# Four graph layers on one core: TensorE's signals moved to drains, and a new order in the second attention

## The chip, the core and the metric

The kernel runs on one core of one Trainium2 chip. A core has TensorE (matmuls, results in PSUM), VectorE, ScalarE and GpSimd for arithmetic, SyncE for issuing transfers, and 16 DMA engines. The engines run their own instruction streams and meet through semaphores: an instruction may wait until a semaphore has reached a number, and may raise one when it is done. The metric is the device time of one execution in microseconds.

## The reference: what is computed

A graph of 6250 nodes with 128 features and 106250 edges (sorted by target) goes through four layers, each followed by a residual and a layer norm:

```python
edge_index = jnp.stack([src, dst])
deg = jnp.maximum(segment_sum(ones(dst.shape), dst), 1.0)
x = _layernorm(x + _L0_gnn_ref(x, ..., deg ** -0.5, src, dst, edge_type_40))  # 40 relations, weights 128x128 each
x = _layernorm(x + _L1_gnn_ref(x, edge_index, W, att_src, att_dst, ...))       # attention, 4 heads of 64
x = _layernorm(x + _L2_gnn_ref(x, edge_index, W_proj, score_src, ...))         # attention, 4 heads of 32
x = _layernorm(x + _L3_gnn_ref(x, edge_index))                                 # 6 rounds of capsule routing
```

The second attention, which the change rearranges, is this:

```python
scores = leaky_relu(s_src[src] + s_tgt[tgt], 0.2)
exp_scores = exp(scores - max(scores))
denom = segment_sum(exp_scores, tgt)
att = exp_scores / (denom[tgt] + 1e-16)
out = segment_sum(proj[src] * att[:, :, None], tgt)
```

## The kernel before

Edges are laid out in 880 chunks of 128 slots, each chunk with targets of one tile of 128 nodes. Work goes by groups of CQ = 4 chunks, so there are NQ = 220 groups, and most buffers are rings of RING = 4 groups. `sweep(eng, stages, ...)` writes one engine's program: for each iteration q it runs the listed steps in their order, a step `(off, fn)` on group q + off. Each engine has its own sweep, and they meet through semaphores alone. A step's waits stand at its head.

Five stages issue indirect transfers from GpSimd, one for each chunk:

- *Relation products* (line 490 on): GpSimd scatters 831 columns of edge records into `rec_tab` (L472). Beside it, TensorE makes y = x W_r for all nodes and 40 relations: for each of 50 tiles a transpose (L491), which ScalarE reads into `xt` (L484), and ten matmuls of 512 columns (L497), each of which VectorE adds into `y_out` (L509) and SyncE stores to `y_tab`. TensorE may be four products ahead of VectorE (`s_yc`).
- *First gather* (`total`, L827): rows of `y_tab` are gathered (L562 `ring<-y_tab`), summed by one-hot matmuls, four a group, and added by VectorE to `acc` (L813). SyncE stores one-hots for later stages.
- *Source maxima* of the first attention: GpSimd gathers (L1035 `ring_m`), ScalarE packs score parts (L1088), TensorE's `turn` transposes them (L1108), ScalarE copies the lines (L1096), TensorE's `spread` makes for each chunk four narrow matmuls (L1118) and a wide one (L1121), and VectorE takes the maximum (L1067). The gathered rows are stored to `k_tab`. GpSimd may reuse a buffer when ScalarE has packed it and the store has landed.
- *Second attention* (`attend_once`): GpSimd gathers (L562 `ring_e<-t_tab`); it may reuse a buffer when VectorE's `message` has read it. `expand` (L1532) and `turn` (L1542) are matmuls on loaded one-hots `ohts`; VectorE's `sent` (L1440) sums the expansion, `score` (L1449, L1451, L1454) ends in `lane_top`; TensorE's `lanes` (L1548) transposes that, VectorE's `top` (L1458, L1461) takes the running maximum, TensorE's `spread_top` (L1552) spreads it, ScalarE's `shift` (L1504, L1507, L1511) negates it and takes the exponentials, VectorE's `message` (L1468) multiplies, TensorE's `total` (L1561) sums the messages by target, and VectorE's four `add` steps (L1484, L1487, L1490) put the sums into `acc`.
- *First routing round*: GpSimd gathers (L1827), SyncE stores the rows, TensorE does `total` (L1963), `turn` (L1953) and `expand` (L1942), VectorE product, sums, shares, messages (L1845 to L1881), ScalarE exponentials and copies (L1904 to L1922).

Between them lie the first attention proper (`attend`) and, at the end, five later rounds (L2060 to L2239), whose transfers are all SyncE's.

On the kernel before, every signal of TensorE is raised by the last matmul of a step, as in

```python
for c in range(CQ):
    last = nc.tensor.matmul(sums(s, c), hots[:, s, c, :], msg[:, s, c, :],
                            start=True, stop=True)
last.then_inc(s_sum, 1)
```

## Time and profile before

| what | value |
|---|---|
| median of 3 runs (lowest to highest) | 11336.08 us (11329.6 to 11339.88) |
| the profiled execution | 11339.56 us |
| its span, first to last instruction | 11337.8 us |
| mean granted clock of TensorE | 0.703 |
| busy: TensorE, VectorE, ScalarE, GpSimd | 60%, 57%, 22%, 57% |

No engine is busy two thirds of the time, so the page's shares alone say little: they are averages over stages with different limits. The profile calls TensorE's matmuls PE, its weight loads PEld, VectorE DVE, ScalarE ACT, GpSimd POOL and the issuing of a queue POOLq or SPq. An idle time is put down to a releaser: an engine and line, a DMA, "issue" (nothing that the profile shows) or "remote" (a signal that it can't match to an instruction's end). Names in rows drop buffer and stage numbers: `ring_e` is that of the second attention in rows of L562.

### The profile page before, as it was taken

The numbers are of one execution on the slowest core, as the hardware profiler recorded it, in microseconds if no ns is written. First come the engines' busy times: TensorE is split into PE (matmuls) and PEld (weight loads), VectorE is DVE, ScalarE is ACT, GpSimd is POOL, SyncE is SP. The second block draws the span as 40 slices with busy tenths as digits, with TensorE's granted clock in tenths as the row PEclk, the third lists the DMA queues.
The fourth block names the chain that finished last, engine by engine and source line by source line (L and its number), as shares of the span: only waits on it lengthen the run. The fifth ranks groups of instructions, "written<-read, shape, count | busy, mean of one in ns | idle before, by whom it ended". The sixth has DMA issues, their size and how long they took to land. (4 is left out here: it accounts for less than half of the span.)

```text
span 11337.8 us, 161595 instructions
## 1 busy us (share of the span) xinstructions
PE 6767.9 (60%) x41381; PEld 5071.3 (45%) x41382; DVE 6482.6 (57%) x18631; ACT 2515.4 (22%) x6766; POOL 6430.9 (57%) x5741
## 2 busy tenths in 40 slices
PE   4422256333337777688745555345444698898986
PEld 3200022333323333344434444244444698898986
DVE  7411135555555555677754444534444688888888
ACT  0000000000010000022211111133333455555554
POOL 0477732777726666444235555255555587787876
PEclk9755577555565555599865555577776899999998
DMA  0111135555546666655322222233333566666664
GB/s 22 58 47 46 46 145 184 117 115 117 113 80 172 176 175 176 167 181 182 115 53 62 61 61 62 40 97 97 95 97 96 145 210 186 186 210 187 209 186 149
DMA packets 1109223, 1395.56 MB, mean 123 GB/s; under 512 B 277691, under 2 KB 974351, under 8 KB 1108111
## 3 DMA queue, kind: packets, MB, share of 16 engines
q1 hardware_dynamic: 955182, 1090.46, 31.1%
q0 software_dynamic: 153312, 296.65, 12.9%
q8 instruction: 304, 4.98, 0.2%
q14 instruction: 425, 3.47, 0.1%
HBM read 1002.58 MB, written 383.96 MB: 122 GB/s over the span
## 5 line engine op out<-in xcount | busy, mean ns | idle before, releaser
L562 POOL DMA_INDIRECT ring_e<-t_tab,src_row x880 | 832.4, 946 | 825.6 <-DVE msg_e L1468 424.1
L1827 POOL DMA_INDIRECT z_r<-x_tab,src_row x880 | 839.4, 954 | 805.6 <-DVE msg_r L1865 405.1
L562 POOL DMA_INDIRECT ring<-y_tab,y_row x880 | 881.7, 1002 | 726.4 <-DVE ring L783 356.5
L472 POOL DMA_INDIRECT rec_tab<-pay,row_i x831 | 842.3, 1014 | 694.5 <-POOLq L202 402.1
L2227 PE MATMUL ps<-u,wide_r 128*128 x9280 | 1141.4, 277 | 126.2 <-issue 88.7
L2239 PE MATMUL ps<-msg_r,hots_r 128*128 128x128 f32 x9280 | 1150.8, 277 | 105.4 <-POOL msg_r L2060 104.7
L2060 POOL TENSOR_TENSOR msg_r<-zo_r,share_r 128x1024 f32<-128x1024 f32 x580 | 1122.8, 1936 | 87.5 <-DVE share_r L2119 13.7
L2227 PEld LDWEIGHTS ps<-u,wide_r 128*128 128x128 f32 x9280 | 1093.0, 194 | 128.2 <-issue 128.2
L2239 PEld LDWEIGHTS ps<-msg_r,hots_r 128*128 128x128 f32 x9280 | 1083.2, 192 | 138.4 <-POOL msg_r L2060 137.7
L1035 POOL DMA_INDIRECT ring_m<-t_tab,src_row x880 | 850.5, 966 | 516.7 <-ACT slot_parts_m L1088 262.9
L497 PE MATMUL ps<-w,xt 128*128 128x512 f32 x1000 | 607.2, 747 | 821.8 <-issue 503.7
L2068 POOL TENSOR_TENSOR prod_r<-prod_r 128x512 f32<-128x512 f32 x580 | 735.1, 1267 | 437.4 <-DVE prod_r L2091 425.1
L509 DVE TENSOR_TENSOR y_out<-ps,rf_b 128x512 f32<-128x512 f32 x500 | 330.9, 689 | 1124.8 <-remote 794.4
L827 PE MATMUL ps<-ring,hots 128*128 128x129 f32 x1760 | 458.6, 442 | 835.4 <-issue 561.1
L1067 DVE TENSOR_REDUCE high_m<-ps 128x4 f32<-128x512 f32 x880 | 588.9, 685 | 623.4 <-PE ps L1121 348.3
L827 PEld LDWEIGHTS ps<-ring,hots 128*128 128x128 f32 x1760 | 394.1, 329 | 900.1 <-issue 679.0
L497 PEld LDWEIGHTS ps<-w,xt 128*128 128x128 f32 x1000 | 207.4, 228 | 1202.8 <-issue 672.4
L1118 PE MATMUL ps<-lines_m,pick_m 48*128 48x128 bf16 x3520 | 530.5, 304 | 350.2 <-DVE high_m L1067 273.5
L2091 DVE TENSOR_TENSOR prod_r<-ps,zo_r 128x1024 f32<-128x1024 f32 x580 | 707.9, 1221 | 33.3 <-PE ps L2227 30.8
L2130 DVE TENSOR_TENSOR u_sum<-ps,u_sum 128x128 f32 x2320 | 667.4, 288 | 89.5 <-PE ps L2239 40.2
L1561 PE MATMUL ps<-msg_e,hots_e 128*128 128x132 f32 x1760 | 468.2, 447 | 333.9 <-DVE msg_e L1468 333.9
L1963 PE MATMUL ps<-msg_r,hots_r 128*128 128x128 f32 x1760 | 341.4, 355 | 509.9 <-DVE msg_r L1865 395.2
(320 smaller groups left out, 13430.4 us busy)
## 6 DMA issues: line engine op xcount, KB each, us to landing
zo_r<-zo_tab SPq DMA_DIRECT2D x2320, 192.0 KB
y_tab<-y_out SPq DMA_DIRECT2D x250, 512.0 KB
k_tab<-ring_m SPq DMA_DIRECT2D x220, 520.0 KB
ring_e<-k_tab SPq DMA_DIRECT2D x220, 520.0 KB
ohts_e<-oht_tab SPq DMA_DIRECT2D x440, 128.0 KB
zo_tab<-z_r SPq DMA_DIRECT2D x220, 256.0 KB
dl_b<-dl_tab SPq DMA_DIRECT2D x220, 128.0 KB
oht_tab<-ohts SPq DMA_DIRECT2D x220, 128.0 KB
```

The source lines that it names most:

```text
L472: nc.gpsimd.indirect_dma_start(out=rec_tab, out_offset=bass.IndirectOffsetOnAxis(ap=row_i[:, j:j + 1], axis=0), in_=pay[:, j, :], in_offse ...
L497: nc.tensor.matmul(ps[:, n % 4, :], xt[:], w0[:, 4 * g:4 * g + 4, :], start=True, stop=True).then_inc(s_y, 1)
L562: nc.gpsimd.indirect_dma_start(out=ring[:, s, c, 0:width], out_offset=None, in_=table, in_offset=bass.IndirectOffsetOnAxis(ap=rows[:, q * ...
L827: last = nc.tensor.matmul(ps[:, (s % 2) * CQ + c, 0:W], hots[:, s, c, :], ring[:, s, c, :], start=True, stop=True)
L1035: nc.gpsimd.indirect_dma_start(out=ring[:, s, c, :], out_offset=None, in_=t_tab, in_offset=bass.IndirectOffsetOnAxis(ap=src_row[:, q * CQ ...
L1827: nc.gpsimd.indirect_dma_start(out=z[:, s, c * D:(c + 1) * D], out_offset=None, in_=x3_tab, in_offset=bass.IndirectOffsetOnAxis(ap=src_row ...
L2060: nc.gpsimd.tensor_tensor(msg[:, g % WR].rearrange("p c (k d) -> p c k d", d=CD), z_of(g).rearrange("p c (k d) -> p c k d", d=CD), share[: ...
L2068: nc.gpsimd.tensor_tensor(prod[:, :, 0:CD // 2], prod[:, :, 0:CD // 2], prod[:, :, CD // 2:CD], ALU.add).then_inc(s_half, 1)
L2091: v.tensor_tensor(prod[:].rearrange("p (c k) d -> p c (k d)", k=CAPS), up, z_of(g), ALU.mult).then_inc(s_prod, 1)
L2130: v.tensor_tensor(t, ps[:, 4 + g % 2, a * D:(a + 1) * D], t, ALU.add)\
L2227: last = nc.tensor.matmul(ps[:, 2 * (g % 2) + c // 4, c % 4 * D:(c % 4 + 1) * D], wide[:, g % WR, c, :], u[:, bass.ds(tiles[g % NO % 4 * O ...
L2239: last = nc.tensor.matmul(ps[:, 4 + g % 2, c // 2 * D:(c // 2 + 1) * D], hots[:, g % WR, c, :], msg[:, g % WR, c, :], start=c % 2 == 0, st ...
```

## The change

It does two things.

First, in the five stages with indirect transfers TensorE's matmuls and transposes raise no semaphore any more. Behind them stands a drain, an instruction of TensorE that raises it: 550 in the relation products (one for each of 50 transposes and 500 products), 220 in the first gather, 5 a group in the source maxima and in the second attention, 3 a group in the first round. The stages without indirect transfers keep their signals.

Second, the second attention is put in another order. TensorE's total runs one group late and stands between this group's `lanes` and `spread_top`; `expand` and `turn` work two groups ahead, not one, and stand last. VectorE's adds are two groups late, not one, and `sent` stands just ahead of `message`. ScalarE does `shift` ahead of `hot`, the latter one group ahead. SyncE loads the one-hots two groups ahead. `spread` is put into another bank of PSUM.

```diff
@@ relation products
-                        nc.tensor.transpose(ps[:, 7, 0:P], xs[:], ident[:]).then_inc(s_xtp, 1)
+                        nc.tensor.transpose(ps[:, 7, 0:P], xs[:], ident[:])
+                        nc.tensor.drain().then_inc(s_xtp, 1)
...
                             nc.tensor.matmul(ps[:, n % 4, :], xt[:], w0[:, 4 * g:4 * g + 4, :],
-                                             start=True, stop=True).then_inc(s_y, 1)
+                                             start=True, stop=True)
+                            nc.tensor.drain().then_inc(s_y, 1)
@@ first gather
-                        last.then_inc(s_sum, 1)
+                        nc.tensor.drain().then_inc(s_sum, 1)
@@ source maxima: turn, spread
-                            nc.tensor.transpose(turned(s), parts[:, s, :], ident_b[:])\
-                              .then_inc(s_turn, 1)
+                            nc.tensor.transpose(turned(s), parts[:, s, :], ident_b[:])
+                            nc.tensor.drain().then_inc(s_turn, 1)
...
-                                                 far[:].rearrange("p h e -> p (h e)"), start=False, stop=True)\
-                                  .then_inc(s_spread, 1)
+                                                 far[:].rearrange("p h e -> p (h e)"), start=False, stop=True)
+                                nc.tensor.drain().then_inc(s_spread, 1)
@@ second attention (attend_once)
                 def spread(s):
-                    return ps[:, 6 + s % 2, 3 * P:3 * P + 1]
+                    return ps[:, (s % 2) * CQ // PER, 3 * P:3 * P + 1]
...
-                        sweep(sp, [(1, hots_in)], straight=True)
+                        sweep(sp, [(2, hots_in)], straight=True)
...
-                        tiles = Tiles(DVE_ENGINE, -1)
+                        tiles = Tiles(DVE_ENGINE, -2)
...
-                        sweep(dve, [(1, sent), (-1, add(0)), (0, score), (-1, add(1)), (-1, add(2)),
-                                    (0, top), (-1, add(3)), (0, message)], tiles, straight=True)
+                        sweep(dve, [(0, score), (-2, add(0)), (-2, add(1)), (0, top), (-2, add(2)),
+                                    (-2, add(3)), (1, sent), (0, message)], tiles, straight=True)
...
-                        sweep(act, [(0, hot), (0, shift)], straight=True)
+                        sweep(act, [(0, shift), (1, hot)], straight=True)
...
-                        tiles = Tiles(PE_ENGINE, 1)
+                        tiles = Tiles(PE_ENGINE, 2)
...
-                            last.then_inc(s_sum, 1)
-                        sweep(pe, [(1, expand), (1, turn), (0, lanes), (0, spread_top), (0, total)], tiles, straight=True)
+                            nc.tensor.drain().then_inc(s_sum, 1)
+                        sweep(pe, [(0, lanes), (-1, total), (0, spread_top), (2, expand), (2, turn)], tiles, straight=True)
```

The other signals of the second attention (`s_exp`, `s_turn`, `s_row`, `s_bc`) and the three of the first round (`s_exp`, `s_turn`, `s_sum`) are moved to a drain in the same way. Line numbers of the changed kernel are one to three higher.

On TensorE, one group in the middle of the second attention stood like this before (`exp_n` with `ohts` is the expansion, which comes four times, `ident_b` the transposes, then lanes, spread and total; drains are no rows here):

```order
L1532 ISA
L1532 MATMUL ps<-exp_n_e2,ohts_e2 128x12
...
L1542 MATMUL ps<-ident_b,ohts_e2 128x128 x4
L1548 MATMUL ps<-ident,lane_top_e2 1x128
L1552 MATMUL ps<-run_top_e2,one_row_e2 128x1
L1561 MATMUL ps<-msg_e2,hots_e2 128x132 x4
```

and stands like this now:

```order
L1550 MATMUL ps<-ident,lane_top_e2 1x128
L1564 MATMUL ps<-msg_e2,hots_e2 128x132 x4
L1555 MATMUL ps<-run_top_e2,one_row_e2 128x1
L1534 ISA
L1534 MATMUL ps<-exp_n_e2,ohts_e2 128x12
...
L1544 MATMUL ps<-ident_b,ohts_e2 128x128 x4
```

The four sums (`msg_e2`, now of the group before) moved from behind the spread to ahead of it, and the expansion from the head to the end.

On VectorE, the same group before (`sent`, an add and its copy, the three of score, further adds, the two of top, the message; repeated adds are left out):

```order
L1440 TENSOR_REDUCE sent_e2<-ps 128x16
...
L1484 SCALAR_TENSOR_TENSOR acc<-acc,fade_e2,ps 128x132
...
L1449 TENSOR_TENSOR sc_e2<-ring_e2,sent_e2 128x16
L1451 SCALAR_TENSOR_TENSOR sc_e2<-sc_e2 128x16
L1454 TENSOR_REDUCE lane_top_e2<-sc_e2 128x1
...
L1487 TENSOR_TENSOR acc<-ps,acc 128x132
...
L1458 TENSOR_REDUCE quad_top_e2<-ps 1x1
L1461 TENSOR_TENSOR run_top_e2<-quad_top_e2,run_top_e2 1x1
...
L1468 TENSOR_TENSOR msg_e2<-ring_e2,msg_e2 128x4x128
```

and now:

```order
L1451 TENSOR_TENSOR sc_e2<-ring_e2,sent_e2 128x16
L1453 SCALAR_TENSOR_TENSOR sc_e2<-sc_e2 128x16
L1456 TENSOR_REDUCE lane_top_e2<-sc_e2 128x1
...
L1486 SCALAR_TENSOR_TENSOR acc<-acc,fade_e2,ps 128x132
...
L1460 TENSOR_REDUCE quad_top_e2<-ps 1x1
L1463 TENSOR_TENSOR run_top_e2<-quad_top_e2,run_top_e2 1x1
...
L1442 TENSOR_REDUCE sent_e2<-ps 128x16
L1470 TENSOR_TENSOR msg_e2<-ring_e2,msg_e2 128x4x128
```

`sent` moved from the head of the group to just ahead of the message, and score is now the first thing behind the message of the group before.

## Rows read from the trace of the kernel before

**Rows 1.** The page's strip of 40 equal slices: TensorE's granted clock, in tenths.

```profile
PEclk9755577555565555599865555577776899999998
```

**Rows 2.** Busy time by stage: PE, PEld, DVE, ACT, POOL, PEclk, DMA share, GB/s.

```profile
405.00:1545.00 1140.00, 339.47 (x442) 106.90 (x442) 143.16 (x208) 11.51 (x44) 842.25 (x831) 0.56 0.16 54
1545.00:1862.00 317.00, 275.54 (x608) 109.24 (x608) 187.74 (x292) 13.59 (x57) 0.00 (x0) 0.97 0.59 242
1896.00:3168.00 1272.00, 458.33 (x1760) 394.08 (x1760) 670.68 (x1754) 0.00 (x0) 881.69 (x880) 0.50 0.53 113
3347.00:4734.00 1387.00, 1015.11 (x4620) 418.14 (x4620) 762.00 (x1993) 90.39 (x441) 850.51 (x880) 0.50 0.65 172
5770.00:7260.00 1490.00, 796.38 (x4180) 638.76 (x4180) 685.28 (x3311) 253.58 (x882) 832.38 (x880) 0.50 0.28 60
7374.00:8894.00 1520.00, 734.84 (x4400) 663.70 (x4400) 630.30 (x1756) 543.33 (x2863) 839.43 (x880) 0.70 0.37 96
```

**Rows 3.** Who GpSimd waited for: us in total, times, longest.

```profile
POOL ring_e L562 <- DVE msg_e L1468: 424.1, 216, 7.1
POOL z_r L1827 <- DVE msg_r L1865: 405.1, 88, 6.8
...
POOL ring_m L1035 <- ACT slot_parts_m L1088: 262.9, 100, 16.3
POOL z_r L1827 <- issue: 257.3, 791, 5.3
...
POOL ring_m L1035 <- issue: 253.7, 780, 3.9
POOL ring_e L562 <- issue: 204.0, 663, 0.5
...
POOL ring L562 <- remote: 109.3, 38, 3.6
```

**Rows 4.** Timeline in the relation products: start, us, instruction, idle before it.

```profile
907.66 0.28 ACT L484 ACTIVATE xt<-ps 128x128 f32<-128x128 f32 x1 [58.33 <-remote]
...
923.07 0.69 DVE L509 TENSOR_TENSOR y_out<-ps,rf_b 128x512 f32<-128x512 f32 x1 [4.91 <-remote]
...
923.81 2.08 PE L497 MATMUL ps<-w,xt 128*128 128x512 f32 x2 [4.18 <-DVE y_out L509]
```

**Rows 5.** Timeline in the first routing round: TensorE's weight loads.

```profile
8029.41 0.19 PEld L1942 LDWEIGHTS ps<-unit,wide_r 128*128 128x128 f32 x1 [1.23 <-issue]
...
8030.82 0.19 PEld L1942 LDWEIGHTS ps<-unit,wide_r 128*128 128x128 f32 x1 [1.23 <-issue]
```

**Rows 6.** Timeline of one group in the second attention.

```profile
6404.70 0.17 DVE L1449 TENSOR_TENSOR sc_e<-ring_e,sent_e 128x16 f32<-128x16 f32 x1
...
6405.34 0.08 PEld L1548 LDWEIGHTS ps<-ident,lane_top_e 128*1 128x1 f32 x1 [1.01 <-DVE lane_top_e L1454]
...
6406.45 0.50 PEld L1552 LDWEIGHTS ps<-run_top_e,one_row_e 1*128 1x128 f32 x2 [1.04 <-DVE run_top_e L1461]
...
6407.07 0.17 ACT L1504 ACTIVATE neg_e<-ps 128x1 f32<-128x1 f32 x1 [5.44 <-issue]
...
6407.80 0.69 DVE L1468 TENSOR_TENSOR msg_e<-ring_e,msg_e 128x512 f32<-128x512 f32 x1 [1.07 <-ACT msg_e L1511]
...
6408.55 2.12 PE L1561 MATMUL ps<-msg_e,hots_e 128*128 128x132 f32 x8 [1.51 <-DVE msg_e L1468]
...
6410.25 0.42 PEld L1532 LDWEIGHTS ps<-exp_n_e,ohts_e 128*128 128x128 bf16 x4
...
6411.32 0.16 DVE L1449 TENSOR_TENSOR sc_e<-ring_e,sent_e 128x16 f32<-128x16 f32 x1
```

**Rows 7.** Timeline in the source maxima: TensorE's narrow and wide matmuls.

```profile
3902.20 0.34 PEld L1118 LDWEIGHTS ps<-lines_m,pick_m 48*128 48x128 bf16 x4 [0.44 <-issue]
...
3902.74 0.61 PE L1121 MATMUL ps<-far_m,others_m 128*128 128x512 bf16 x1
...
3903.28 0.34 PEld L1118 LDWEIGHTS ps<-lines_m,pick_m 48*128 48x128 bf16 x4 [0.44 <-DVE high_m L1067]
```

More of the change, by code:

```diff
@@ L1535, in expand @@
                                     start=True, stop=True)
-                            last.then_inc(s_exp, 1)
+                            nc.tensor.drain().then_inc(s_exp, 1)
                         def turn(q, s):
@@ L1543, in turn @@
                                                            ohts[:, s, c * P:(c + 1) * P], ident_b[:])
-                            last.then_inc(s_turn, 1)
+                            nc.tensor.drain().then_inc(s_turn, 1)
                         def lanes(q, s):
                             pe.wait_ge(s_lt, q + 1)
-                            nc.tensor.transpose(lane_row(s), lane_top[:, s, :], ident[:]).then_inc(s_row, 1)
+                            nc.tensor.transpose(lane_row(s), lane_top[:, s, :], ident[:])
+                            nc.tensor.drain().then_inc(s_row, 1)
                         def spread_top(q, s):
                             pe.wait_ge(s_rt, q + 1)
-                            nc.tensor.matmul(spread(s), one_row[:], run_top[0:1, s:s + 1], start=True, stop=True)\
-                              .then_inc(s_bc, 1)
+                            nc.tensor.matmul(spread(s), one_row[:], run_top[0:1, s:s + 1], start=True, stop=True)
+                            nc.tensor.drain().then_inc(s_bc, 1)
                         def total(q, s):
@@ L1945, in expand @@
                                             start=True, stop=True)
-                                    last.then_inc(s_exp, 1)
+                                    nc.tensor.drain().then_inc(s_exp, 1)
                                 def turn(q, s):
@@ L1954, in turn @@
                                                                    ohts[:, s, c * P:(c + 1) * P], ident_b[:])
-                                    last.then_inc(s_turn, 1)
+                                    nc.tensor.drain().then_inc(s_turn, 1)
                                 def total(q, s):
@@ L1964, in total @@
                                                                 msg[:, s, c * D:(c + 1) * D], start=True, stop=True)
-                                    last.then_inc(s_sum, 1)
+                                    nc.tensor.drain().then_inc(s_sum, 1)
                                 sweep(pe, [(-1, total), (1, turn), (2, expand)], tiles, straight=True)
```

## The prediction

> **What bounds the kernel now.** I first read the page's strip of 40 slices, then cut the span into stages, then asked each stage which engine's waits add up to its length. Five stages issue indirect transfers from GpSimd, and the granted clock of TensorE is low just there [rows 1]. They take 1140 + 317 us (relation products, with the scatter of the records and after it), 1272 (first gather), 1387 (source maxima), 1490 (second attention) and 1520 us (first routing round) [rows 2]: 7126 of 11337.8 us. In each, GpSimd does the same thing: 880 gathers, or 831 scatters, of 0.95 to 1.01 us busy each (the busy sums in [rows 2] over their counts), about 0.3 us of issue between them, and waits for others [rows 3]. Busy time, issue and waits make 850.5 + 253.7 + 262.9 = 1367 us in the source maxima, 832.4 + 204.0 + 424.1 = 1460 in the second attention and 839.4 + 257.3 + 405.1 = 1502 in the first round. A wait that vanished would leave the usual 0.3 us, so 100, 216 and 88 waits leave 233, 359 and 379 us to win, and the first gather's 38 of 109.3 us leave 98. The floor is then 1134, 1101 and 1123 us, for 220 groups of four transfers each 5.0 to 5.2 us. That floor is the first thing to keep in mind.
>
> The second is what holds it up. In the relation products VectorE adds 29 tiles of ten in the 317 us behind the scatter and only 21 in the 1140 us beside it (608 and 442 TensorE records, 21 to a tile) [rows 2]. At 923 us it has waited 4.91 us for a product and works 0.69 on it, 5.6 us for each; TensorE starts another product at 923.81, 0.05 us after that add ended, so VectorE's signals are prompt and TensorE is ready ahead; ScalarE sat 58.33 us before it could read one transpose at 907.66 [rows 4]. So the signals of matmuls arrive late, in a queue. In the first round TensorE's own loads step slowly: 8029.41 to 8030.82 is 1.41 us for a load and a matmul, 0.7 us for each [rows 5]; 5.6 us is eight such steps. The second attention has no such delay: there ScalarE starts at 6407.07, 0.62 us after the load of the tiny matmul it reads, in every group alike, and the 6.62 us of a group (6404.70 to 6411.32) is a plain chain [rows 6].
>
> **Drains.** 50 + 500 signals in the relation products, 220 in the first gather, 1100 in the source maxima, 1100 in the second attention and 660 in the first round move from the matmul to a drain behind it: 3630 drains. No row shows one. What they can take away are the late signals; what they cost is overlap, since the next weights may load only when the array is empty. 
> - *Relation products.* When signals are prompt a tile takes about 11 us: 29 in 317 us [rows 2]. Fifty are 550 us, half of the 1140 us that GpSimd scatters in. The stage then ends with the scatter and the 317 us behind it go. Bounds: 0 (delay stays) to 365 (842.3 us busy and 0.3 us between 831 scatters are 1092 us, 48 less than the 1140). I take 317.
> - *First gather.* One signal a group; VectorE's 670.68 us and TensorE's 458.33 are 3.0 and 2.1 us a group and fit under 5.2 [rows 2]. Bounds 0 to 98, taken 98.
> - *Source maxima.* Four spreads a group, each four narrow matmuls and a wide one, 1.08 us apart; from the first load to the wide one's end is 3902.20 to 3903.35, 1.15 us [rows 7]. With a drain the next load starts behind that end; I add 0.1 us for the drain, estimated from the 0.05 us in which a signalled engine starts, twice. TensorE is busy 1015 us or 4.6 a group [rows 2], so the transpose takes some 0.3 beside four times 1.08. Four times 1.25 and 0.4 make 5.4 us: TensorE, at its lower level here (granted 0.50, 1.2 GHz), becomes the limit over GpSimd's 5.15. 220 x 5.4 = 1188 against 1367: 175 taken, bounds 0 (6.2 us a group, drains of 0.3 us) and 233.
> - *First round.* 379 us of waiting. TensorE is busy 734.84 us in 220 groups, 3.3 us each, at a mean grant of 0.70; all at the low level (0.50) that would be 4.7, with three drains 5.0 [rows 2]. GpSimd's 5.1 stays the limit, near a tie: 355 taken, bounds 0 and 379.
>
> Here a rule speaks against the change. In the second attention a total's next load starts 1.70 us after the total's first load (6408.55 to 6410.25) though the matmuls end at 2.12 [rows 6]: 0.4 us of overlap that a drain takes. The Trainium skill, page "TensorE: Matmul & The Clock Gate", section "Single matmul latency", gives about 183 ns at the low clock for what a matmul hides when others follow; by it 3630 drains would take 660 us of TensorE time, by the row's 0.4 us 1450. Neither is added, because except in the source maxima it lies under GpSimd.
>
> **The second attention's new order.** Before, on one chain: score, lanes' transpose, top, spread, ScalarE's three, message, sums (2.12 us), expansion, `sent`, score. After, the sums of q-1 run on TensorE behind the lanes of q, the expansion is a group ahead. The loop, by [rows 6]: score to the transpose's load 0.64 (6404.70 to 6405.34); transpose 0.37; drain 0.1; sums 2.12; drain 0.1; spread to ScalarE 0.62 (6406.45 to 6407.07) and 0.03; ScalarE to message 0.73; message to the next score 0.61 (0.69 less the overlap of neighbours). That is 5.3 us. `quad_top`, `run_top` and the adds lie beside the 2.12 of the sums (VectorE is busy 3.1 us a group in all [rows 2]); the next group's transposes and expansions follow the spread and lie beside ScalarE and the message. 220 x 5.3 = 1166 us against 220 x 6.62 = 1456: 290 taken. Bounds: 359 (GpSimd's floor) and 200 (drains at 0.25 us each: 5.7 us a group). The gather transfers wait for the message of three groups ago and will be asked for at once; the loads of `ohts` come one group earlier with four buffers, 128 KB each, at a DMA share of 0.28.
>
> **Sum.** 317 + 98 + 175 + 355 + 290 = 1235 us. The profiled execution took 11339.56 us around a span of 11337.8, and the median is 11336.08, 0.03% lower. 11339.6 - 1235 = 10105, so 10100 us.
>
> **The rivals.**
> - *All prompt, as above* (0.60): 9900 to 10400.
> - *Cured in part* (0.20): delays stay where TensorE does most per signal and stores are heavy. For it: in the relation products each matmul advances by 0.7 us steps, which a drain need not change. Relation products and first round unchanged give 10100 + 317 + 355 = 10770; the source maxima alone, 10275. Range 10400 to 10900.
> - *Drains don't touch the delay, only the new order counts* (0.10): 11340 - 290 = 11050, 10900 to 11310. For it: in [rows 5] the loads themselves, which raise nothing, are late, so completion as such may be slow, with or without a signal.
> - *Slower* (0.07): the drain waits for the same slow completion, and now everything behind it on TensorE stands still. The Trainium skill, page "PSUM — Partial Sum Buffer", section "Engine vs sequencer instructions", says that drain waits for the engine to go fully idle. One delay of 0.7 us per drain serial in source maxima and first round, where groups have 5 and 3: 220 x (5 + 3) x 0.7 = 1230 us on top of 5.4 and 5.1 us, thus 8.9 and 7.2 us a group against 6.2 and 6.8 now; +590 and +90, less 290: 11730. It decides where 290 us are lost against now: 0.33 us for each of the 880 spreads, over the 0.16 that brings a group of the maxima from 5.4 back to 6.2.
> - *Nothing measurable* (0.03): order's gain and drains' loss cancel.
>
> **How the numbers follow.** The likeliest is 10100. Its case and the partial cure hold 8 in 10, so the range is 9900 to 10900. The low end is all five floors: 11340 - 365 - 98 - 233 - 359 - 379 = 9906. 0.2% is 23 us, about what a measurement tells from no change. Faster 0.90, same 0.03, slower 0.07.
>
> **What would show it.** Relation products ending within some 20 us of the last scatter; VectorE's 4.9 us waits gone; ScalarE's 58 us waits gone. GpSimd at 5.0 to 5.3 us a group in all but the source maxima, and there TensorE's loads following each wide matmul by 0.1 us, a group in 5.4. In the second attention a group in 5.3 us with the sums between the lanes' transpose and the spread. From 8925 us on (the later rounds) nothing changes its length. Wrong: loads on TensorE that still step by 0.7 or 1.4 us beside indirect transfers; a drain that delays the next load by more than 0.3 us; or transfers that take longer once they are asked for sooner (the source maxima already have a DMA share of 0.65).

## The result and the profile after

The changed kernel takes **11408.82 us** (median of 5 runs, 11395.09 to 11430.54), the kernel before 11339.88 us beside it (5 runs, 11329.6 to 11344.11). The ratio is 1.0063, with a 95% interval of 1.0049 to 1.0077: 0.6% slower, where 10100 us had been forecast.

One thing has to be known for the numbers below. The experiments ran on several chips, and the kernel before took 11342 to 11347 us on some of them (11340 beside the change), but 10247 to 10253 us on others. One chip of each kind was used two times, some 40 minutes apart, and was of the same kind both times. So every experiment is read against the kernel before on its own chip, and I call the two kinds **late chips** and **prompt chips**, for what their traces turned out to show.

First the stages of the profile after, in the columns of [rows 2]. Its span is 11428.4 us; the profiled execution was the slowest of the five, 22 us over their median, so the stages add up to somewhat more than the medians differ by:

```profile
405.00:1542.00 1137.00, 412.76 (x419) 101.64 (x420) 137.49 (x199) 11.10 (x42) 829.28 (x831) 0.51 0.15 52
1542.00:1949.00 407.00, 353.37 (x632) 94.70 (x631) 208.07 (x302) 14.07 (x59) 0.04 (x1) 0.96 0.47 194
1983.00:3250.00 1267.00, 456.13 (x1760) 394.25 (x1760) 668.69 (x1754) 0.00 (x0) 882.95 (x880) 0.50 0.52 114
3426.00:4856.00 1430.00, 1053.85 (x4590) 415.61 (x4590) 799.77 (x1973) 89.31 (x440) 837.27 (x881) 0.50 0.61 167
5904.00:7390.00 1486.00, 931.04 (x4180) 694.64 (x4180) 686.15 (x3309) 253.87 (x881) 832.37 (x880) 0.50 0.26 60
7508.00:8981.00 1473.00, 948.47 (x4388) 788.77 (x4389) 636.97 (x1752) 542.90 (x2862) 836.07 (x880) 0.57 0.38 99
```

Against [rows 2], the work behind the scatter grew from 317 to 407 us, and the first gather (1267) and the second attention (1486) stayed where they were. The windows have margins of some us, so the stages' costs are better taken from the starts of GpSimd's first transfers in them, of before in the first line view and of after in the second (count, minimum, median and maximum in ns, first and last start):

```profile
L562 POOL DMA_INDIRECT ring<-y_tab,y_row x880: 942/947/1362, 1896.9 to 3147.5; - x176
L1035 POOL DMA_INDIRECT ring_m<-t_tab,src_row x880: 943/949/3143, 3347.3 to 4712.9; - x176
L562 POOL DMA_INDIRECT ring_e<-t_tab,src_row x880: 942/947/1004, 5770.4 to 7229.9; - x176
L1827 POOL DMA_INDIRECT z_r<-x_tab,src_row x880: 942/947/1467, 7374.0 to 8874.9; - x176
```

```profile
L564 POOL DMA_INDIRECT ring<-y_tab,y_row x880: 942/947/1382, 1983.6 to 3233.9; - x176
L1037 POOL DMA_INDIRECT ring_m<-t_tab,src_row x880: 943/949/3147, 3426.6 to 4824.9; - x176
L564 POOL DMA_INDIRECT ring_e<-t_tab,src_row x880: 942/947/997, 5904.5 to 7365.5; - x176
L1830 POOL DMA_INDIRECT z_r<-x_tab,src_row x880: 942/947/1449, 7507.9 to 8962.5; - x176
```

The lag of after behind before is 86.7, 79.3, 134.1 and 133.9 us at these four starts and 90.6 at the end of the span. So the relation products cost 87 us, the first gather gives 7, the source maxima (with what follows up to the second attention) cost 55, the second attention gives nothing and the first round 43. Of the five terms of the sum, 317, 98, 175, 355 and 290, none arrived.

The reason is in the waits of the profile after (us in total, times, longest), where PEq is TensorE's sequencer and PEq L500, L1111, L1125 and L1556 are the new drains:

```profile
DVE y_out L511 <- PEq L500: 1121.9, 465, 20.0
ACT lines_m L1098 <- PEq L1111: 1075.2, 174, 21.9
...
ACT neg_e L1506 <- PEq L1556: 801.6, 126, 7.3
...
DVE high_m L1069 <- PEq L1125: 533.1, 667, 13.8
...
POOL ring_e L564 <- DVE msg_e L1470: 351.0, 109, 8.3
...
POOL z_r L1830 <- DVE msg_r L1868: 326.8, 136, 8.0
```

VectorE still waits for the products, only that the wait now ends with the drain. The drains themselves stand in the views of their lines, with minimum, median and maximum in ns:

```profile
L500 PEldq DRAIN  x500: 942/1100/6198, 422.3 to 1945.8; - x167
```

```profile
L1566 PEldq DRAIN  x220: 1925/2102/5147, 5933.5 to 7386.2; - x110
```

A drain behind a product lasts 1.10 us where all is well and up to 6.2 where it isn't; one behind the sums of the second attention, which are 2.10 us of matmuls, up to 5.1. A drain waits for the late completion like everyone else. (A matmul's end is modelled in the profile, so no row tells whether the array works slowly or finishes in time and reports late. "Late completion" stands for both.)

The second attention shows when that happens. Before, nothing was late there. The timeline after, of two groups (start, us, instruction, idle before it):

```profile
6502.99 0.95 POOL L564 DMA_INDIRECT ring_e<-t_tab,src_row  x1 [3.71 <-DVE msg_e L1470]
...
6503.87 2.10 PE L1564 MATMUL ps<-msg_e,hots_e 128*128 128x132 f32 x8 [0.23 <-DVE acc L1486]
...
6506.05 0.50 PEld L1555 LDWEIGHTS ps<-run_top_e,one_row_e 1*128 1x128 f32 x2 [0.38 <-issue]
...
6506.74 0.95 POOL L564 DMA_INDIRECT ring_e<-t_tab,src_row  x1 [0.31 <-issue]
...
6508.38 0.95 POOL L564 DMA_INDIRECT ring_e<-t_tab,src_row  x1 [0.69 <-issue]
...
6510.12 2.10 PE L1564 MATMUL ps<-msg_e,hots_e 128*128 128x132 f32 x8 [0.23 <-DVE acc L1489]
...
6512.13 0.96 POOL L564 DMA_INDIRECT ring_e<-t_tab,src_row  x1 [0.31 <-issue]
...
6513.73 0.49 PEld L1555 LDWEIGHTS ps<-run_top_e,one_row_e 1*128 1x128 f32 x2 [1.82 <-issue]
...
6516.13 0.94 POOL L564 DMA_INDIRECT ring_e<-t_tab,src_row  x1 [3.04 <-DVE msg_e L1470]
```

In the first group GpSimd has just paused 3.71 us; the sums end at 6505.97 and TensorE goes on at 6506.05. The loop is then the one that was forecast: 5.4 us from message to message. In the second, GpSimd's four transfers follow the last four after only 0.69 us; the sums end at 6512.22, but the next load starts at 6513.73, 0.6 us after GpSimd's last transfer of that run ended (6513.09), and the group takes 7.7 us. Then GpSimd has to wait for messages (3.04 us), and the next group is prompt again. Through most of the stage groups of 5.4 us alternate with late ones of 7.7 to 8.4, and their mean is the old 6.6 us.

Counted over all 220 drains of L1566: where at most four transfers had begun in the 8 us before the drain did (104 drains), the mean is 2.1 us; with five (58 drains) it is 4.1 and with six (58) 3.3. In the first gather the same count gives 2.07 us for the 66 drains with at most four, and 5.1, 5.9 and 9.1 us for the 154 with five, six and seven. It is no rule for the whole kernel: of the drains behind products (L500), the eight with three or four such transfers took 3.8 to 5.5 us, so what went before counts too (experiment 9 comes back to it).

**Theory A**, from this: on such a chip TensorE's completions come late, drain or not, while GpSimd issues indirect transfers one behind the other, and short pauses in them keep it from happening. Where TensorE is late, GpSimd soon has to wait, and that is its pause: the stages settle at the length at which GpSimd pauses enough, whatever is won in their chains. **Theory B**, the rival: the drains themselves bring the lateness into the second attention.

### The profile page after: what moved, and what is told of

The parts are those of the page before. It is cut to its first block and busy times, and to the rows that moved or that the text cites. A ratio compares the mean times of both kernels' runs of the same rounds, so it can differ in the third digit from the quotient of the medians.

```text
span 11428.4 us, 165225 instructions
## 1 busy us (share of the span) xinstructions
PE 7313.4 (64%) x41381; PEld 5234.5 (46%) x41382; DVE 6549.6 (57%) x18631; ACT 2518.2 (22%) x6766; POOL 6402.9 (56%) x5741
## 5 line engine op out<-in xcount | busy, mean ns | idle before, releaser
L2242 PE MATMUL ps<-msg_r,hots_r 128*128 128x128 f32 x9280 | 1152.3, 277 | 104.9 <-POOL msg_r L2063 104.3
L498 PE MATMUL ps<-w,xt 128*128 128x512 f32 x1000 | 746.9, 837 | 689.8 <-issue 655.0
L1204 POOL TENSOR_TENSOR msg_e<-ring_e,msg_e 128x768 f32<-128x768 f32 x220 | 324.1, 1473 | 558.0 <-ACT msg_e L1310 558.0
L2182 ACT ACTIVATE wide_r<-zo_r 128x1024 f32<-128x1024 uint8 x580 | 605.5, 1044 | 86.1 <-PE ps L2230 60.2
```

Source lines behind the costliest of these rows:

```text
L498: nc.tensor.matmul(ps[:, n % 4, :], xt[:], w0[:, 4 * g:4 * g + 4, :], start=True, stop=True)
L2242: last = nc.tensor.matmul(ps[:, 4 + g % 2, c // 2 * D:(c // 2 + 1) * D], hots[:, g % WR, c, :], msg[:, g % WR, c, :], start=c % 2 == 0, st ...
```

## The experiments

**1. The order alone.** No drain anywhere; the edit on the kernel before is the order's part of the change:

```diff
-  sweep(pe, [(1, expand), (1, turn), (0, lanes), (0, spread_top), (0, total)], ...)
+  sweep(pe, [(0, lanes), (-1, total), (0, spread_top), (2, expand), (2, turn)], ...)
```

> The kernel before with the second attention's new order and no drain. Theory A (GpSimd's indirect transfers, once they follow each other without a pause of some 1.7 us, make TensorE's completions late, with a drain or without): the faster order lets GpSimd close its pauses, completions become late in about every second group, and the stage keeps 1440 to 1480 us; the total is within 40 us of before. Theory B (the drains make the delay in the second attention): groups of 5.3 us, the stage 1170 to 1200 us, the total about 11050.

This met a prompt chip: 9913.43 us against 10253.16 (ratio 0.9675, 0.9659 to 0.9691). There the second attention takes what GpSimd needs and no more:

```profile
405.00:1476.00 1071.00, 472.92 (x1050) 185.75 (x1050) 322.49 (x500) 24.84 (x101) 795.84 (x831) 0.74 0.34 129
1512.00:2663.00 1151.00, 447.71 (x1740) 389.69 (x1741) 665.89 (x1739) 0.00 (x0) 880.62 (x880) 0.50 0.56 124
2855.00:3991.00 1136.00, 954.04 (x4471) 412.53 (x4558) 783.28 (x1962) 88.18 (x435) 852.31 (x880) 0.50 0.77 208
5048.00:6169.00 1121.00, 729.09 (x4132) 616.09 (x4132) 682.33 (x3254) 250.06 (x870) 848.93 (x880) 0.50 0.34 79
6306.00:7446.00 1140.00, 705.87 (x4372) 650.55 (x4372) 624.50 (x1731) 538.10 (x2835) 860.48 (x880) 0.79 0.49 127
```

All 50 tiles of products are done beside the scatter (x1050), and each gather stage runs at GpSimd's floor of 5.1 to 5.2 us a group. These are the floors of the forecast, without a single drain. On its own this run can't part A from B: on a prompt chip nothing is late. The granted clock is 0.50 (the 1.2 GHz level) in three of the five rows here too, so the low clock is not what makes completions late.

**2. The drains alone**, in the old order (prompt chip).

```diff
-  sweep(pe, [(0, lanes), (-1, total), (0, spread_top), (2, expand), (2, turn)], ...)
+  sweep(pe, [(1, expand), (1, turn), (0, lanes), (0, spread_top), (0, total)], ...)
```

> The kernel after with the second attention's old order; all 3630 drains stay. Theory A: relation products, source maxima and first round as in the kernel after (88 and 54 us longer, 46 us shorter than before); the second attention keeps GpSimd's pause of about 1.9 us in each group, so no completion is late there, and its chain grows by five drains of about 0.05 us: 6.62 to 6.9 us a group, 1460 to 1515 us. Total 11400 to 11490. Theory B: the second attention shows late completions here too, over 7 us a group.

10608.03 us against 10253.16 (1.0352, 1.0335 to 1.0370): no lateness (every drain of L1566 lasts 2.13 us), but drains are dear in themselves. The source maxima take 1206 us, 5.5 a group, and the second attention 1704, which is 7.7 a group in place of 6.6. I had expected 0.05 us a drain. A group now takes 7.5 us, and every fourth 8.6. TensorE in one of the plain groups:

```profile
6011.72 1.82 PEld L1564 LDWEIGHTS ps<-msg_e,hots_e 128*128 128x128 f32 x8 [1.62 <-DVE msg_e L1470]
...
6014.17 0.48 PEld L1534 LDWEIGHTS ps<-exp_n_e,ohts_e 128*128 128x128 bf16 x4 [0.63 <-issue]
```

From the sums' first load to the expansion's it is 2.45 us, where it was 1.70 [rows 6]. The sequencer sets registers for each of the expansion's four matmuls; before, it did so from 0.13 us after the sums' start on (6408.68), beside them, and now it does so when the drain of 2.13 us has ended, and the four matmuls take 0.56 us in place of 0.30. Every fourth group has one instruction of the sequencer more there:

```profile
L591 PEldq TENSOR_LOAD <-chunk_tile x1: 1109/1109/1109, 6005.3 to 6005.3; - x1
```

In that group the sums start at 6003.10; the sequencer waits in the drain, loads the next tile numbers into its registers at 6005.3 for 1.11 us, and the expansion starts at 6006.72, 3.62 us after the sums. The old order without drains has this load too, in one group of four, and takes the same 1.92 us from the sums' first matmul to the expansion's with the load and without: there it is hidden behind the sums. So of the 1.1 to 1.2 us that a group grows by, some 0.9 come with the drains in every group, and 0.3 are the load of 1.11 us in one of four.

**3. Two probes with drains**: half the gathers of the second attention are left out from the fifth group on, and the scatters wait behind the products.

```diff
-  for c in range(CQ):                              # gathers, second attention
+  for c in range(2 if q >= RING else CQ):
...
   def _(pool):                                     # relation products
+      pool.wait_ge(s_y, NTP * GRP)
```

> The kernel after with two probes. In the second attention GpSimd issues only two of a group's four gathers from the fifth group on (half of the gathered rows are left out, so the sums are of stale rows); in the relation products GpSimd's scatters wait until all products are made. Theory A: with two gathers a group GpSimd pauses 2.8 us in every group, so no completion is late and the new order shows its own loop of 5.3 to 5.4 us, the stage 1170 to 1200 us; the products take 11 us a tile from the first to the last, 550 us for 50, and behind them the scatters take 831 x 1.265 = 1050 us. Theory B (drains as such): every second group of the second attention still takes 7.7 us, and products with a drain stay at 58 us a tile part of the time.

Prompt chip again, 10767.5 us (one run). The new order's own loop with drains is 1235 / 220 = 5.6 us: 5.4 in three groups and 6.2 to 6.4 in every fourth, the one with the load of tile numbers. Products with drains take 654 us in all, 12.8 a tile, over the 11 that I had expected.

**4. Pauses in the scatter alone.**

```diff
   for j in range(EJ):
+      if j % 4 == 0 and 0 < j // 4 * 7 <= NTP * GRP:
+          pool.wait_ge(s_yc, j // 4 * 7)
```

> The kernel before with one edit in the relation products: after every fourth scatter GpSimd waits until seven more products are added, as long as there are products. Theory A: four scatters are 5.1 us and seven products 7 to 8 us, so GpSimd pauses 2 to 3 us in every such stretch, no completion is late, 50 tiles take 500 to 550 us with about 285 scatters beside them, and the 546 left take 690 us: the stage is 1200 to 1240 us in place of 1455, total 11080 to 11130. If it is the mere presence of indirect transfers or of the stores beside them that makes completions late, products stay slow, GpSimd waits for them, and the stage is over 2000 us.

On the prompt chip this only costs: 10424.02 against 10253.16 (1.0172, 1.0155 to 1.0189), the stage 1244 us. The trace also shows the old order of the second attention on a prompt chip: 6.6 us a group, as on the late chip of [rows 6]. So nothing was late there in the old order on either kind.

**5. The kernel after again**, unchanged (late chip).

> The kernel after, unchanged, beside the kernel before. The kernel before took 10253 us in the experiments so far, against 11340 beside the first run of the kernel after, and no completion was late in them. Theory C: late completions belong to the machine the kernels run on, not to the kernel. If before takes about 10250 here, after shows no late completion, the source maxima take 1205 us (70 longer than without drains), the second attention 1230 us, and the total is 10080 to 10120, 1.5% under before. If before takes about 11340, after is 11400 again, with the stages of its first profile. Rival: late completions come with the kernel after's drains as such; then after is above 11300 even where before takes 10250.

11429.09 against 11341.89 (1.0081, 1.0064 to 1.0098), with GpSimd's stages starting within 9 us of where they did in the first profile. So the result on record is that of a late chip. The kernel after was never run on a prompt one; from stages that were, counted from stage start to stage start, it would be 9913 less 10 (first gather), plus 77 (source maxima) and 11 (first round) as between experiments 1 and 2, plus 116 (second attention, between 1 and 3): about 10107 against 10250. That is a sum over three traces, not a run.

**6. Order and pauses, without drains** (the same late chip).

> Two edits on the kernel before: the second attention's new order without drains, and in the relation products GpSimd waits for seven more added products after each four scatters. Theory C with no late completions (before at about 10250): the order gives 335 us, the pauses cost 170 as in the run of the pauses alone, total 10085. With late completions (before at about 11340) and theory A: the pauses keep the products at 11 us a tile and the stage at 1240 us in place of 1455, the second attention closes GpSimd's pauses and stays at 1440 to 1480 us, total 11100 to 11150. If late completions need no dense transfers, the relation products stay slow and the total is over 11500.

11083.0 against 11341.89 (0.9772, 0.9756 to 0.9789). Its two stages:

```profile
405.00:1645.00 1240.00, 471.86 (x1050) 184.81 (x1050) 322.04 (x500) 24.90 (x101) 798.34 (x831) 0.71 0.30 112
5551.00:6980.00 1429.00, 730.57 (x4137) 617.30 (x4138) 676.58 (x3260) 250.41 (x870) 832.27 (x880) 0.50 0.27 63
```

With GpSimd made to pause, all 50 tiles are made beside the scatter, as on a prompt chip: 1240 us in place of 1457. And the order without a single drain still takes 1429 us where the prompt chip takes 1121: groups of 4.7 and 5.4 us alternate with late ones of 6.9 to 8.4. Theory B falls: lateness comes into the second attention with the faster order, not with the drains. Of the 290 us forecast for the order, 61 arrive without drains (1490 to 1429), and the drains take them away again (1486 in the profile after).

**7. The probes of 3 without drains** (the same late chip).

> No drains, the second attention's new order with two of four gathers a group left out from the fifth group on (its sums are of stale rows), and the scatters behind the relation products. The same two probes with drains gave 1234 us (5.6 us a group) in the second attention and 11 to 13 us a tile of products. If the drains on the chain hold the new order's loop, it is faster without them: 4.7 to 5.0 us a group, 1030 to 1100 us. With late completions about (before at about 11340) and theory A, both probes are prompt all the same, since GpSimd pauses; if completions are late here too, the pauses don't cure.

Both were prompt. The rows (all products in 532 us with no transfer about; two gathers a group, 1080 us or 4.9 a group):

```profile
405.00:937.00 532.00, 473.09 (x1050) 188.04 (x1050) 319.65 (x498) 24.96 (x101) 0.00 (x0) 0.97 0.62 254
5915.00:6995.00 1080.00, 728.93 (x4131) 615.91 (x4131) 672.61 (x3250) 249.96 (x870) 423.84 (x448) 0.50 0.22 56
```

The same loop without drains is 0.7 us a group shorter than in experiment 3.

**8. Shorter pauses, and drains in the first round** (late chip): the kernel of 6 with six products in place of seven, and the drains of L1949, L1958 and L1968.

> The kernel before with three edits: the second attention's new order without drains, drains in the first routing round alone, and in the relation products GpSimd waits for six more added products after each four scatters (a period of 6.2 to 6.6 us, a pause of 1.2 to 1.5). On a machine with late completions (before at about 11340), by theory A: if a pause of 1.2 to 1.5 us is still enough, the relation products take 1190 to 1210 us (1240 with seven), and the total is 11000 to 11040 with the first round's 46 us; if it is too short, the products are late in part and the stage is 1250 to 1450. On one without (before at about 10250): order -335, pauses +120, drains +10, total 10050.

10967.95 against 11347.04 (0.9666, 0.9653 to 0.9679). The relation products' stage is 1184 us, so shorter pauses, most of them of 0.7 to 2 us, are enough; the first round takes 1453 us in place of the 1520 of [rows 2] without drains. The whole is 32 us under the range that I had expected.

**9. Doses of pauses** (the same late chip as 8). Before scatter j GpSimd waits for the count of added products in a table:

```diff
+  for n, a in [(4, 7), (4, 6), (4, 5), (8, 12), (8, 10), (16, 21)]:
+      for k in range(1, 78 // a + 1):
+          waits[j0 + k * n] = a0 + k * a
+      j0, a0 = j0 + 78 // a * n, a0 + 78 // a * a
...
+      if j in waits:
+          pool.wait_ge(s_yc, waits[j])
```

> How long a pause, after how many transfers. No drains. In the relation products GpSimd's scatters wait in six stretches of 75 to 78 products each: four scatters to seven products, four to six, four to five, eight to twelve, eight to ten, sixteen to twenty-one (prompt products take 1.0 us each, a scatter 1.27, so the pauses are about 2.2, 1.2, 0.4, 2.2, 0.3 and 1.1 us). In the second attention (new order) GpSimd waits before every second group alone and then issues eight gathers in a row. Theory A with late completions about (before at 11340): the stretches with the pauses of 2.2 us are prompt (7.2 us and 12.5 us a period), those with 0.3 to 0.4 us fall to 5.6 us a product; the pause of 1.2 us lies near the edge, prompt if over half of 1.7. In the second attention the pause is per eight gathers: if the run of eight stays prompt, a group takes 5.8 us or less (1280 us), else 6.5 as before (1430). If late completions depend on the share of time and not on the pause, four to seven and eight to twelve differ from four to six alone by their share (5.1 of 7.2, 10.1 of 12.5, 5.1 of 6.2).

VectorE's busy time and count of adds in the six stretches and in the one without waits behind them:

```profile
424.00:506.00 82.00, 48.81 (x77) 0.99 0.61 241
506.00:587.00 81.00, 50.49 (x79) 0.98 0.65 252
587.00:675.00 88.00, 49.07 (x76) 0.96 0.59 228
675.00:756.00 81.00, 46.43 (x72) 0.98 0.61 241
756.00:840.00 84.00, 44.94 (x70) 0.90 0.55 214
840.00:917.00 77.00, 40.94 (x64) 0.93 0.55 214
917.00:1166.00 249.00, 44.00 (x65) 0.62 0.20 71
```

Per product that is 1.06, 1.03, 1.16, 1.13, 1.20, 1.20 and, without waits, 3.8 us. I had expected four to five and eight to ten to be late all through; they lose a tenth or two. The doses that GpSimd took are not those of the table, though. Where the products ran ahead of the count it didn't wait at all: the trace has runs of 20 transfers in the stretch of four to five and one of 26 in that of eight to ten, with prompt products for the most part, then some late ones, then a pause of 5 to 10 us in which TensorE caught up. A late product makes GpSimd wait for it, which is a pause: a wait on the neighbour's own progress heals itself. How long a pause has to be after how many transfers, this run doesn't tell.

What it does show is that lateness builds up. The last of the waits ends at 918 us. For 19 us more the products stay prompt beside unbroken transfers, and then they fall behind:

```profile
918.00:937.00 19.00, 11.95 (x20) 1.00 0.66 257
...
962.00:1166.00 204.00, 26.80 (x39) 0.58 0.15 51
```

That is 0.95 us a product and 5.2. In the kernel before it was the same: the scatters start at 405.7 us, and the products are prompt until 446. Once late, they are not brought back by one short pause. Before, in the middle of the stage:

```profile
693.47 0.69 DVE L509 TENSOR_TENSOR y_out<-ps,rf_b 128x512 f32<-128x512 f32 x1 [4.92 <-remote]
...
697.12 0.96 POOL L472 DMA_INDIRECT rec_tab<-pay,row_i  x1 [2.97 <-issue]
...
699.06 0.69 DVE L509 TENSOR_TENSOR y_out<-ps,rf_b 128x512 f32<-128x512 f32 x1 [4.90 <-remote]
```

GpSimd paused 2.97 us there, and the next products still came 5.6 us apart. So theory A holds in this form: pauses that come again and again, set by the neighbour's progress, keep TensorE from falling behind.

In the second attention, eight gathers in a row and then one wait took 1454 us against 1429: nothing won over four.

**10. Transfers or any work?** Two kernels. In one, plain multiplications on GpSimd stand ahead of the scatters, and in the second attention one of four gathers is left out; in the other (the rested kernel), the kernel of 8 has such a multiplication behind each group's gathers, in the second attention and the first round.

```diff
+  for j in range(500):
+      ...
+      nc.gpsimd.tensor_tensor(fill[:, j % 2], fill[:, 2], fill[:, 2], ALU.mult)
...
   for c in range(CQ):
       nc.gpsimd.indirect_dma_start(...).then_inc(s_gath[s], 16)
+  pool.wait_ge(s_fill, q + 1)
+  nc.gpsimd.tensor_tensor(fill[:, 0], fill[:, 1], fill[:, 1], ALU.mult).then_inc(s_fill, 1)
```

> Is it GpSimd's work or its indirect transfers? No drains. In the relation products GpSimd first runs 500 multiplications of a 128 x 384 scratch tile back to back (near 1 us each, nobody reads them), and its scatters follow behind them; in the second attention (new order) three of four gathers of a group are issued from the fifth group on (its sums are of stale rows). Theory A, that transfers without a pause do it: all 50 tiles of products are prompt, 10.1 to 11 us each, 510 to 550 us in all, and in the second attention three transfers leave a pause of over 1 us in a group of 5 us: 1080 to 1130 us. Rival: any dense work of GpSimd does it, then the products fall to 5.6 us each within 30 us of its start (over 2000 us for the stage). If three transfers a group are already too dense, the second attention takes 1200 to 1400 us. Where before takes about 10250, neither theory is tested by the first probe.

> The kernel of three edits (new order, drains in the first round alone, four scatters to six products) with one more: in the second attention and in the first round GpSimd multiplies a 128 x 384 scratch tile, near 1 us, after each group's four gathers, so that a group takes it 6.1 to 6.2 us at the least. Theory A, with late completions about: 1.2 us without a transfer in every 6.2 is what kept the products prompt, so both stages run at 6.15 to 6.3 us a group, 1355 to 1385 us in place of 1427 and 1451, total 10830 to 10900 against 10968. If only an idle GpSimd cures, or a pause of 1.2 us is too short here, the multiplication is only added: 1430 to 1500 and 1450 to 1550, total 10970 to 11100. Without late completions (before at about 10250) it costs 220 x 1.0 us in each, some 440 in all.

On two prompt chips (the second time with 750 multiplications ahead of the scatters in place of 500) they answered nothing but their cost. The one with multiplications ahead took 10259.3 and 10444.85 us, one run each. The rested kernel takes 10294.4 against 10249.92 and 10296.26 against 10247.18, 1.0042 and 1.0048 (0.5% more); the new order alone had taken 9913.43 on such a chip, so its pauses, with the first round's drains, cost some 380 us there. Then both ran on a late chip:

> The rested kernel a third time, since it has met only machines without late completions (10295, before at 10250). With late completions (before at about 11340), theory A: the second attention and the first round run at 6.0 to 6.2 us a group, 1320 to 1370 us each in place of 1427 and 1451, total 10780 to 10870 against 10968. If only an idle GpSimd cures or the pause is too short, the work is only added and the total is 10970 to 11100.

> The probes of the longer filler again, for a machine with late completions (before at about 11340). Theory A: products prompt, 10 to 11 us a tile, beside 590 us of GpSimd's multiplications without a pause; second attention with three gathers a group 1075 to 1130 us if the pause of 1.3 us is enough. Rival, that any dense work of GpSimd delays completions: products fall to 5.6 us each.

The one with multiplications ahead of the scatters (11163.88 us, one run):

```profile
405.00:938.00 533.00, 473.22 (x1050) 187.59 (x1050) 320.04 (x499) 24.94 (x101) 532.91 (x680) 0.97 0.62 254
5973.00:7055.00 1082.00, 729.38 (x4133) 616.33 (x4134) 674.03 (x3255) 250.28 (x870) 626.13 (x664) 0.50 0.30 69
```

GpSimd is busy 532.91 of 533 us and every product is prompt: it is the indirect transfers and not GpSimd's work. Three gathers a group are prompt as well (4.9 us).

The rested kernel takes **10756.88 us** against 11345.35 (0.9485, 0.9469 to 0.9501), the fastest on a late chip. Its second attention and first round:

```profile
5483.00:6792.00 1309.00, 732.30 (x4131) 616.69 (x4131) 817.57 (x3250) 250.03 (x870) 1033.47 (x1101) 0.50 0.30 68
6928.00:8285.00 1357.00, 925.63 (x4352) 770.19 (x4352) 693.59 (x1731) 537.80 (x2835) 1042.51 (x1101) 0.60 0.40 106
```

GpSimd has 0.84 us more to do in each group, and the stages are 120 and 96 us shorter than in experiment 8 (1429 and 1453). That is 5.95 and 6.2 us a group. It is no full cure: on a prompt chip the second attention of the same kernel takes 5.7 us in nearly every group; here one group in five still takes over 6.9. The total is 23 us under the range that I had expected.

## Why the prediction was wrong, step by step

**The step that failed** is "I take the signal to be prompt, because the delay sits in matmul completions and the drain makes the sequencer raise it". The first half holds and contradicts the second: if completions are late, whatever waits for completion is late. The drain waits for the array to be idle, and in the profile after it lasts up to 6.2 us behind one product. The Trainium skill, page "PSUM — Partial Sum Buffer", section "Engine vs sequencer instructions", has just this rule; the trace agrees (2.10 us behind 2.10 us of sums, and longer where they are late). I had it in the slower rival with 0.07, and [rows 5], quoted in the third rival, said it too: loads that raise nothing were late.

- *Relation products*, -317: measured +87. Nothing was cured; VectorE's adds beside the scatter fell from 208 to 199. Behind it, 30 tiles at 13.5 us (407 us over 632 / 21) replace 29 at 11.0. That is a cost that I had set to nothing. It shows without any lateness too: 12.8 us a tile with drains in experiment 3 and 10.3 without in experiment 7. A product with a drain can't overlap the next load.
- *First gather*, -98: measured -7. The size was right: the stage takes 1151 and 1141 us without and with drains on a prompt chip, 100 and more under the late chip's. But it is the chip that decides it, not the drain.
- *Source maxima*, -175: measured +55. The 5.4 us a group with TensorE as the limit was right where nothing is late: 1206 / 220 = 5.5, with the spreads 1.23 us apart (1.25 in the forecast). On the late chip it comes on top of the lateness. (1188 from 1367 is 179, not 175; it changes nothing.)
- *First round*, -355: measured -43. Drains do help here (and alone, in experiment 8). They don't cure: GpSimd still waits 327 us for messages, of 405. Why they help at all stays open.
- *Second attention*, -290: measured nothing. "No such delay: in every group alike" was read rightly from [rows 6], but its cause not asked for. GpSimd paused 1.9 us in every group (424 us over 216 waits, [rows 3]), and that pause kept TensorE prompt. The faster order takes the pause away. The loop itself was sized nearly right: 5.4 us in the prompt groups after, against 5.3; with half the gathers its mean was 5.6, for the load of tile numbers in every fourth group, which the sum had left out.
- *GpSimd's waits as time to win*: that was the structural error. On a late chip the waits are no slack but what keeps the stage going. The floors of 5.0 to 5.2 us a group are real, and reached on prompt chips without any drain. The forecast had no room for two kinds of chips; the profile before shows one of them alone.

Of the rivals, the third had the mechanism right for the drains ("completion as such may be slow"), but gave the order its 290 us all the same. The fourth said slower, by the right rule, at too high a price: it put the source maxima at 8.9 us a group, the first round at 7.2 and the whole at 11730, where 6.5, 6.7 and 11409 came. One late step of 0.7 us for each drain did not come, since most drains in the source maxima are prompt (of the 880 of L1125, with a median of 1.12 us, 194 took over 1.29). It too gave the order its 290 us.

**What stays open**: what on the late chips couples GpSimd's indirect transfers to TensorE's completions, and why some chips do it and others don't. The Trainium skill, page "DMA: Bandwidth & Descriptors", section "SWDGE vs HWDGE vs iDMA", says that such a transfer's descriptors are written to rings in SBUF by GpSimd; whether these writes are what TensorE waits behind, no run here shows. Nor does any run show how lateness builds up over the first 19 to 40 us of transfers, or what length of pause undoes it. The stores to HBM beside the transfers are not needed for it: the second attention has none.

## What to carry to other kernels

Before a wait is counted as something to win, ask what the pause behind it does for the neighbours: here an engine's idle 1.9 us kept another engine prompt, and of the 290 us that the shorter chain was to bring, 61 came without drains and none with them. A drain is no cure for late completions, for it waits for completion itself; and it keeps the sequencer from working ahead of the array (2.45 us from the sums to the expansion in place of 1.70, and 3.62 where a register load stands between them). And a pause that is placed by hand can be worth more than a shorter chain: with the relation products, the second attention and the first round paced, the new order, and drains in the first round, the kernel is 5% faster on a late chip. On a prompt chip the same kernel is 0.5% slower than before and 3.8% slower than the new order alone, so measure on more than one chip.

## What the runs showed of the hardware

- Two kinds of chips: the same kernel takes 11340 us on some and 10250 us on others, with granted clocks of 0.703 and 0.73 over the span. The difference lies beside GpSimd's indirect transfers: of the 719 us between the two profiles of the kernel with multiplications ahead of the scatters, all but some 14 are in the first gather, the source maxima and the first round.
- On the slower kind, a fp32 product of 128 x 512 completes every 1.0 us for the first 19 to 40 us of unbroken indirect transfers, and every 5.6 us after that. It completes every 1.0 us all through beside no transfers, beside plain GpSimd work, and beside runs of four transfers with pauses between them, most of 0.7 to 2 us (1184 us for the stage in experiment 8).
- The granted clock of TensorE was 0.51 (the lower level nearly throughout) in the relation products of the profile after, where completions were late, and was 0.97 over the whole stage in experiments 7 and 10, where they were prompt.
- A load of tile numbers by TensorE's sequencer takes 1.11 us. Behind four fp32 sums it was hidden (1.92 us to the next matmul with it and without); behind a drain it was not (3.62 us against 2.46).
